# The setup of a two-layer attention kernel: laid-out weights, a bias network in 4 pieces, bias lines by head group on two DMA queues

## The chip, the cores and the metric

One core of a Trainium2 chip. The metric is the device time of one execution in microseconds, the median over several runs; for a changed kernel it is set against runs of the kernel before on the same chip. A profile comes from one more execution.

## The reference

The input x is 8 elements of 256 channels by 32 x 32 positions (1024), all in fp32. Two layers follow each other.

```python
# layer 0, per element, 8 heads of 32 channels
xn   = (x - mean_c(x)) / sqrt(var_c(x) + eps) * gamma
q, k, v = split(w_qkv @ xn)                         # 256 x 1024 each
sim  = einsum('bhdi,bhdj->bhij', q, k) * scale + bias[None]
out0 = w_out @ (softmax(sim) @ v) + x
# the bias depends on the weights alone: a small network on relative positions
rel  = sign(rel) * log(abs(rel) + 1)                # (i, j, 2), 63 x 63 distinct pairs
h    = leaky(rel @ w0.T + b0); h = leaky(h @ w1.T + b1)   # 64 wide
bias = h @ w2.T + b2                                # 8 heads
# layer 1: one head, 1024 x 1024 scores, then a residual
f, g, hh = Wf @ x + bf, Wg @ x + bg, Wh @ x + bh
out  = gamma1 * (hh @ softmax(f.T @ g)) + x
```

## The kernel before

The core works through the 8 elements one after the other (`element(b, ...)` on each engine). An element has two groups of 4 heads, and a group has a rows phase of 32 tiles (PE: scores of 128 x 1024, L617 and L618; DVE: adds the bias and takes the minimum of the negated sum, L1037; ACT: exp with a sum, L836) and a columns phase of 32 tiles (L638, L1051, L853, L665). Layer 1 of the element before, and the normalisation and the k and q of group 0 of the next element, are laid between these tiles by hand-written tables. Each engine executes its instructions in program order, and semaphores join them.

q and k are each split into a high and a low part (ACT writes the high, DVE the low part into `st`), stored to DRAM (`q_out`, `k_out`) and loaded again in another layout (`q_in`, 6 DMAs; `k_in`, 3 DMAs). `st` is a single buffer: `high_q0` may only write after the k store has landed, and `high_k` of group 1 only after the q store of group 1. All DMAs are issued by SP, in one queue and one order.

The bias of a tile is read from `bias_lines` in SBUF, which is filled once, in the setup that this case is about:

1. SP loads x of element 0 and 22 weight tensors. PE transposes the weights (27 products, `tiles_to_turn`) and DVE copies them out of PSUM, with gamma multiplied into `wqkvT` (L884 to L898).
2. The bias network runs on 63 x 63 = 3969 relative positions in `MSTEPS = 9` pieces of 441 columns: three products on PE (L678, L685, L692), two bias additions on ACT (L816, L823), two leaky steps and a table write on DVE (L1005, L1012, L1017). At fixed steps the statistics of element 0 are put in between: mean and var products (L443, 4 each), centre, square, rstd, norm.
3. SP stores the table of 8 heads x 3969 to DRAM (L383), and then writes 32 "lines" (L387, DRAM to DRAM): line x holds, for 8 heads and 63 offsets, the 32 values that column x needs, 504 rows of 128 bytes. After the 17th, SP issues the k store of group 0, and after the 32nd the q store, then `k_in`, `q_in` and 32 loads of bias lines into SBUF (L396, 4 for each head). Beside this PE makes k and q of group 0 (`k0`, `q0`, L486).
4. PE makes its first tiles when `q_in` has landed; DVE takes the first when the four bias loads of head 0 have landed. SP's next entries are the q store and `q_in` of group 1, x of element 1, and the k store of group 1.

## Time and profile before

| | |
|---|---|
| median of 3 runs | 1823.52 us (1823.15 to 1825.76) |
| profiled execution, its own time | 1826.01 us |
| its span | 1824.2 us |
| mean granted clock of PE, as a share of full | 0.928 |
| busy: PE, DVE, ACT | 89%, 82%, 76% of the span |
| DMA | 122.48 MB, almost all on SP's queue |

An engine's share is a mean over the span; a setup and eight elements lie in it. "PEclk" is the clock that PE was granted, as a share of 2.4 GHz; it has the two levels 1.0 and 0.5. A product of fp32 operands appears in the profile as two MATMUL entries. The time of one execution is 1.8 us above its span.

### The profile page before, as it was taken

The page shows a single profiled execution, that of the slowest core. Times are in us where ns is not written, and L with a number is a line of the kernel's source. Part 1 is how long each engine was busy: PE and PEld are TensorE (multiplying, and loading weights), DVE is VectorE, ACT ScalarE, POOL GpSimd, SP SyncE. Part 2 cuts the span into 40 slices and gives each one's busy share as a digit, 9 for nine tenths or more (in the row PEclk, how much of TensorE's full clock was granted, in tenths as well). Part 3 has the DMA queues.
Part 4 walks back from the last instruction along what each step waited for, and adds up shares of the span by engine and source line. Part 5 has one row for each costly group of instructions (what it writes and reads, how often), then busy time and mean ns, then how long its engine had stood idle before and what let it go on. Part 6 is the DMA issues. An engine that isn't in the chain of part 4 may idle for free.

```text
span 1824.2 us, 18855 instructions
## 1 busy us (share of the span) xinstructions
PE 1617.4 (89%) x6033; PEld 762.3 (42%) x6033; DVE 1498.5 (82%) x2217; ACT 1387.4 (76%) x2043; POOL 0.2 (0%) x4
## 2 busy tenths in 40 slices
PE   6635889989998999989998999989998999989988
PEld 2123333535444453534444353534444353535424
DVE  4226889889898989889898989889898988889853
ACT  1215888888788888878888787878788787889753
POOL 0000000000000000000000000000000000000000
PEclk8657878999999999999999999999999999989999
DMA  1298022502034102502034102502034111500000
GB/s 59 57 207 211 1 59 70 151 1 58 16 113 116 51 9 83 159 3 58 4 125 116 47 13 74 158 12 59 1 111 133 36 23 63 144 15 1 26 22 23
DMA packets 59031, 122.48 MB, mean 67 GB/s; under 512 B 22507, under 2 KB 25131, under 8 KB 58923
## 3 DMA queue, kind: packets, MB, share of 16 engines
q1 hardware_dynamic: 58932, 121.28, 24.3%
q8 instruction: 48, 0.79, 0.2%
q14 instruction: 51, 0.41, 0.1%
HBM read 78.66 MB, written 44.13 MB: 67 GB/s over the span
## 4 chain that ended last, share of the span: by engine, by line
PE 51%; DVE 24%; issue 17%; DMA 3%; ACT 3%; SPq 2%; DVEq 0%; ACTq 0%
DVE biased L1037 13%; PE psum L563 9%; PE psum L638 9%; PE psum L665 8%; PE psum L617 6%; PE psum L443 5%; DVE biased L1051 5%; PE psum L618 4%; PE psum L486 3%; PE psum L520 2%; PE psum L496 1%; SPq L387 1%; DMA q_parts<-st 1%; ACT probs L853 1%; DVE probs L971 1%
## 5 line engine op out<-in xcount | busy, mean ns | idle before, releaser
L1037 DVE CUSTOM_DVE_ANT_0 biased<-psum,bias_lines_sb 128x1024 f32<-128x1024 f32 x512 | 617.0, 1222 | 161.4 <-PE psum L618 125.0
L836 ACT ACTIVATE biased<-biased,nmax 128x1024 f32<-128x1024 f32 x512 | 587.2, 1147 | 144.0 <-DVE nmax L1037 139.9
L1051 DVE TENSOR_TENSOR biased<-psum,bias_lines_sb 128x1024 f32<-128x1024 f32 x512 | 598.4, 1218 | 43.5 <-PE psum L638 32.5
L853 ACT ACTIVATE probs<-biased 128x1024 f32<-128x1024 f32 x512 | 536.5, 1056 | 127.1 <-DVE biased L1051 107.5
L638 PE MATMUL psum<-q_stack,k_stack 98*128 98x512 f32 x1024 | 393.6, 492 | 38.8 <-DVE nmax L1037 16.2
L617 PE MATMUL psum<-k_stack,q_stack 96*128 96x512 f32 x512 | 331.3, 647 | 89.5 <-DVE nmax L1037 48.4
L638 PEld LDWEIGHTS psum<-q_stack,k_stack 98*128 98x128 f32 x1024 | 179.2, 201 | 326.8 <-issue 152.8
L665 PE MATMUL psum<-probs,vT 128*32 128x512 f32 x2048 | 283.0, 622 | 6.1 <-DVE st L926 3.9
L617 PEld LDWEIGHTS psum<-k_stack,q_stack 96*128 96x128 f32 x512 | 100.2, 196 | 274.0 <-DVE nmax L1037 175.2
L618 PE MATMUL psum<-k_stack,q_stack 96*128 96x512 f32 x512 | 212.1, 414 | 0.0
L563 PE MATMUL psum<-probs 128*128 128x512 f32 x384 | 186.6, 592 | 0.0
L618 PEld LDWEIGHTS psum<-k_stack,q_stack 96*128 96x128 f32 x512 | 102.7, 201 | 50.6 <-issue 47.3
L486 PE MATMUL psum<-xn,wqkvT 128*128 128x512 f32 x128 | 77.3, 698 | 26.3 <-DVE st L920 15.3
L836 ACT ACTIVATION_READ_ACCUMULATOR biased<-biased,nmax 128x1 f32 x512 | 96.1, 188 | 0.0
L563 PEld LDWEIGHTS psum<-probs 128*128 128x128 f32 x384 | 72.6, 189 | 46.4 <-issue 36.1
L665 PEld LDWEIGHTS psum<-probs,vT 128*32 128x32 f32 x2048 | 42.4, 109 | 101.3 <-issue 74.4
L784 ACT ACTIVATE probs<-probs,nmax 128x1024 f32<-128x1024 f32 x48 | 54.9, 1144 | 16.4 <-DVE probs L983 15.6
L443 PE MATMUL psum<-xn,wqkvT 128*128 128x512 f32 x128 | 66.8, 603 | 0.0
L496 PE MATMUL psum<-wqkvT,xn 128*128 128x256 f32 x256 | 65.7, 378 | 0.0
L532 PE MATMUL psum<-whT,x 128*128 128x256 f32 x256 | 65.5, 380 | 0.0
L508 PE MATMUL psum<-o,woutT 128*128 128x512 f32 x128 | 64.4, 593 | 0.8 <-ACT o L805 0.8
L563 PE MATMUL psum<-o,probs 128*128 128x512 f32 x128 | 64.8, 592 | 0.0
(86 smaller groups left out, 1148.2 us busy)
## 6 DMA issues: line engine op xcount, KB each, us to landing
k_stack<-k_parts SPq DMA_DIRECT2D x48, 512.0 KB, 7.3
q_stack<-q_parts SPq DMA_DIRECT2D x96, 256.0 KB, 5.7
k_parts<-st SPq DMA_DIRECT2D x16, 1024.0 KB, 4.5
q_parts<-st SPq DMA_DIRECT2D x16, 1024.0 KB, 3.9
xn<-in_x_dram SPq DMA_DIRECT2D x8, 1024.0 KB, 8.2
x<-in_x_dram SPq DMA_DIRECT2D x8, 1024.0 KB, 9.1
out_dram<-x SPq DMA_DIRECT2D x8, 1024.0 KB, 4.1
bias_lines_sb<-bias_lines SPq DMA_DIRECT2D x32, 240.0 KB, 23.7
```

The costliest lines, as they stand in the source:

```text
L443: mm = pe.matmul(psum[0:rows, bank + half, :], lhsT(k), src[:, k, half * HALF:(half + 1) * HALF], start=(k == 0), stop=(k == KC - 1))
L486: mm = pe.matmul(psum[:, bank, :], wqkvT[:, k, t * C:t * C + P], xn[:, k, half * HALF:(half + 1) * HALF], start=(k == 0), stop=(k == KC - 1))
L496: mm = pe.matmul(psum[:, 4 + arg % 2, 0:C], xn[:, k, arg * P:(arg + 1) * P], wqkvT[:, k, 2 * C:3 * C], start=(k == 0), stop=(k == KC - 1))
L563: mm = pe.matmul(psum[:, 4 + 2 * c + half, :], hs[:, t % HS, c * P:(c + 1) * P], attn1[t % 3][:, half * HALF:(half + 1) * HALF], start=(t ...
L617: pe.matmul(psum[:, bank, :], lhsT, back(keys, 0, HALF, N), start=True, stop=True)
L618: pe.matmul(psum[:, bank + 1, :], lhsT, back(keys, HALF, HALF, N), start=True, stop=True).then_inc(SEMS["a_mm"], 1)
L638: mm = pe.matmul(psum[:, bank + i, :], k_stack[:, g, 2 * j + i, t * P:(t + 1) * P], q_stack[:, g, NHALF - 1 - half, 2 * j + i, ::-1], star ...
L665: mm = pe.matmul(psum[h * HD:(h + 1) * HD, 4 + half, :], vT[:, t, (g * HG + h) * HD:(g * HG + h + 1) * HD], probs[:, ((q - PV_LAG) * HP + ...
L836: nc.scalar.activation(biased[:, m % BIASED, :], biased[:, m % BIASED, :], ACT.Exp, scale=-1.0, bias=nmax[:, m:m + 1], accum_out=rowsum[:, ...
L853: nc.scalar.activation(probs[:, n % P_SLOTS], biased[:, n % BIASED, :] .rearrange("p (i n) -> p i n", i=2), ACT.Exp).then_inc(SEMS["probs_ ...
L1037: nc.vector.tensor_tensor_reduce(biased[:, m % BIASED, :], pair(bank_of(g, first, ("rows", m))), bias_lines[:, g * HG + h, a0:a0 + N], -1. ...
L1051: nc.vector.tensor_tensor(biased[:, n % BIASED, :].rearrange("p (i n) -> p i n", i=2), psum[:, bank:bank + 2, :], bias_lines[:, g * HG + 2 ...
```

## The change

The host lays the weights out as the products want them (`laid_out`), so that the transposes and their copies are gone; only the product with gamma stays on DVE, now in place on `wqkvT` (two instructions of 128 x 768). The bias network works on two halves of the positions at once: 2 x 64 = 128 partitions with block-diagonal weights (`twice`), 4 pieces of 504 columns. The two halves share the middle row of offsets, and the table is stored in two DMAs. Lines are kept by group of 4 heads (`lines_dram[g, x]`, 252 rows of 128 bytes each): those of group 0 are issued half by SP and half by ACT, those of group 1 all by SP, after the bias loads of group 0. ACT now issues the later constants at the start, its 16 lines, and the k and q stores and loads of group 0 of element 0. The memset of two rows of `k_stack` goes from DVE to GpSimd. Nothing is changed in the elements but that the DMA helpers take the issuing engine as an argument.

```diff
-    lines_dram = nc.dram_tensor("bias_lines", [W, G * HG, DY, W], F32)
+    lines_dram = nc.dram_tensor("bias_lines", [G, W, HG, DY, W], F32)
...
-        MSTEPS = 9
-        MC = DY * DX // MSTEPS
+        HPT = G * HG
+        MROWS = (DY + 1) // 2
+        MSTEPS = 4
+        MC = MROWS * DX // MSTEPS
...
+        def lines_out(eng, g, x, done):
+            src = table_dram.ap().rearrange("h (a w) -> h a w", w=DX)[g * HG:(g + 1) * HG, :, W - 1 - x:2 * W - 1 - x]
+            eng.dma_start(lines_dram.ap()[g, x], src).then_inc(done, 16)
...
         def _(sp):
+            sp.dma_start(mlp, mlp_in).then_inc(mlp_loaded, 16)
+            sp.dma_start(rel_sb, rel_in).then_inc(mlp_loaded, 16)
             sp.dma_start(xn[:], x_dram[0]).then_inc(x_loaded, 16)
+            sp.dma_start(wqkvT[:], wqkv_in).then_inc(weights_loaded, 16)
+            sp.dma_start(gamma_col[:], gamma_in).then_inc(weights_loaded, 16)
...
             sp.wait_ge(table_ready, MSTEPS)
-            sp.dma_start(table_dram.ap(), table_sb).then_inc(table_stored, 16)
-            sp.wait_ge(table_stored, 16)
+            sp.dma_start(table_dram.ap()[:, 0:MROWS * DX], table_sb[0:HPT]).then_inc(table_stored, 16)
+            sp.dma_start(table_dram.ap()[:, MROWS * DX:DY * DX],
+                         table_sb[HPT:2 * HPT, DX:MROWS * DX]).then_inc(table_stored, 16)
+            sp.wait_ge(table_stored, 32)
+            for x in range(0, W, 2):
+                lines_out(sp, 0, x, lines_stored)
+            sp.wait_ge(lines_stored, 16 * W)
+            bias_in(0)
             for x in range(W):
-                src = table_dram.ap().rearrange("h (a w) -> h a w", w=DX)[:, :, W - 1 - x:2 * W - 1 - x]
-                sp.dma_start(lines_dram.ap()[x], src).then_inc(lines_stored, 16)
-                if x == W // 2:
-                    k_out(0, 0)
-            q_out(0, 0)
-            k_in(0, 0)
-            q_in(0, 0, ("s_mm", -1, SN))
-            sp.wait_ge(lines_stored, 16 * W)
+                lines_out(sp, 1, x, late_lines_stored)
+            sp.wait_ge(late_lines_stored, 16 * W)
+            bias_in(1)
...
         def _(pe):
-            pe.wait_ge(weights_loaded, 16 * N_WEIGHTS)
-            pe.wait_ge(consts_set, 1)
-            turned = 0
-            for src in tiles_to_turn((wq_raw, wo_raw, wh_raw), (wf_raw, wg_raw), (w0_raw, w1_raw, w2_raw)):
...
-            pe.wait_ge(rel_loaded, 16)
+            pe.wait_ge(mlp_loaded, 32)
...
         def _(act):
             nc.scalar.preload_act_table_set("natural_log_exp_and_others")
+            n = 0
+            for dst, src in ((ident[:], ident_in), (woutT[:], wout_in), (whT[:], wh_in), (wfgT[:], wfg_in),
...
+            do("rstd", 0, 0, 1, True, False)
+            do("rstd", 1, 0, 1, True, False)
+            act.wait_ge(table_stored, 32)
+            for x in range(1, W, 2):
+                lines_out(nc.scalar, 0, x, lines_stored)
             for kind, arg in (("high_k0", 0), ("high_k0", 1), ("high_q0", 0), ("high_q0", 1)):
                 do(kind, arg, 0, 1, True, False)
+                if (kind, arg) == ("high_k0", 1):
+                    k_out(nc.scalar, 0, 0)
+            q_out(nc.scalar, 0, 0)
+            k_in(nc.scalar, 0, 0)
+            q_in(nc.scalar, 0, 0, ("s_mm", -1, SN))
+            act.wait_ge(consts_loaded, 16 * N_CONSTS)
```

The first place is SP's queue between the table store and x of element 1. `bias_table` is the table in DRAM, `bias_lines` the lines there, `bias_lines_sb` those in SBUF. In the kernel before it reads:

```order
L383 DMA bias_table<-bias_lines_sb 8x3969
L387 DMA bias_lines<-bias_table 504x32 x17
L335 DMA k_parts<-st 128x2x1024
L387 DMA bias_lines<-bias_table 504x32 x15
L335 DMA q_parts<-st 128x2x1024
L362 DMA k_stack<-k_parts 32x4x1024 x3
L348 DMA q_stack<-q_parts 32x4x512 x6
L396 DMA bias_lines_sb<-bias_lines 32x1920 x32
L335 DMA q_parts<-st 128x2x1024
L348 DMA q_stack<-q_parts 32x4x512 x6
L407 DMA xn<-in_x_dram 128x2x1024
```

The same stretch of SP's queue in the changed kernel, where `probs` holds the table in SBUF:

```order
L367 DMA bias_table<-probs 8x2016
L368 DMA bias_table<-probs 8x1953
L330 DMA bias_lines<-bias_table 252x32 x16
L362 DMA bias_lines_sb<-bias_lines 32x1920 x16
L330 DMA bias_lines<-bias_table 252x32 x32
L362 DMA bias_lines_sb<-bias_lines 32x1920 x16
L298 DMA q_parts<-st 128x2x1024
L311 DMA q_stack<-q_parts 32x4x512 x6
L387 DMA xn<-in_x_dram 128x2x1024
```

The stores and loads of k and q of group 0 have left the queue; the q store of group 1 stands behind the lines and bias loads of group 1.

The second place is ACT between the end of the network and the first tile. L749 and L745 are `high_k0` and `high_q0`, L836 is the exp of a tile. Before:

```order
L823 ACTIVATE bias_lines_sb<-psum,probs 64x441 x2
L749 ACTIVATE st<-psum 128x512 x2
L745 ACTIVATE st<-psum 128x512 x2
L836 ACTIVATE biased,rowsum<-biased,nmax 128x1024 x4
L755 COPY vT<-psum 128x256
```

And in the changed kernel, where L716 and L712 are rstd, L732 and L728 are `high_k0` and `high_q0`, and L829 is the exp:

```order
L716 ACTIVATE o<-psum,eps_col 128x1024
L712 ACTIVATE o<-o 128x1024
L330 DMA bias_lines<-bias_table 252x32 x16
L732 ACTIVATE st<-psum 128x512 x2
L298 DMA k_parts<-st 128x2x1024
L728 ACTIVATE st<-psum 128x512 x2
L298 DMA q_parts<-st 128x2x1024
L325 DMA k_stack<-k_parts 32x4x1024 x3
L311 DMA q_stack<-q_parts 32x4x512 x6
L829 ACTIVATE biased,rowsum<-biased,nmax 128x1024 x4
```

ACT now issues 16 lines between rstd and the first `high_k0`, and 11 DMAs for k and q before its first tile.

## Rows read from the trace of the kernel before

**Rows 1.** The page: span, and busy time of the engines.

```profile
span 1824.2 us, 18855 instructions
...
PE 1617.4 (89%) x6033; PEld 762.3 (42%) x6033; DVE 1498.5 (82%) x2217; ACT 1387.4 (76%) x2043; POOL 0.2 (0%) x4
```

**Rows 2.** Stretches: length, busy us (entries) by engine, PEclk, DMA share, GB/s.

```profile
20.70:67.60 46.90, 45.42 (x70) 9.32 (x70) 20.75 (x31) 14.85 (x22) 0.00 (x0) 0.65 0.00 0
...
71.30:84.50 13.20, 4.03 (x9) 1.48 (x7) 1.38 (x2) 1.19 (x2) 0.00 (x0) 0.76 0.49 72
...
108.00:123.50 15.50, 2.07 (x4) 1.16 (x4) 0.05 (x1) 0.00 (x0) 0.00 (x0) 0.50 1.05 219
...
411.00:617.00 206.00, 191.15 (x748) 92.43 (x744) 183.35 (x270) 171.50 (x254) 0.00 (x0) 0.98 0.23 67
```

**Rows 3.** Timeline of ACT and DVE: start, us, what, [idle before, releaser].

```profile
89.20 0.60 ACT L745 ACTIVATE st<-psum 128x512 fp32r<-128x512 f32 x1 [14.96 <-DMA k_parts<-st]
...
123.45 1.22 DVE L1037 CUSTOM_DVE_ANT_0 biased<-psum,bias_lines_sb 128x1024 f32<-128x1024 f32 x1 [27.67 <-DMA bias_lines_sb<-bias_lines]
...
157.35 1.23 DVE L916 TENSOR_TENSOR st<-psum,st 128x1024 fp32r<-128x1024 f32 x1 [6.21 <-ACT st L741]
...
171.35 1.23 DVE L1037 CUSTOM_DVE_ANT_0 biased<-psum,bias_lines_sb 128x1024 f32<-128x1024 f32 x1 [7.21 <-PE psum L618]
```

**Rows 4.** Timeline of PE, same columns.

```profile
13.82 5.42 PE L437 MATMUL psum<-ident,probs 128*128 128x128 f32 x27 [13.82 <-DMA bfg<-in_L_conv_bg_dram]
...
46.91 0.95 PE L678 MATMUL psum<-bias_lines_sb,probs 2*64 2x441 f32 x2
47.79 0.95 PE L685 MATMUL psum<-bias_lines_sb,probs 64*64 64x441 f32 x2
...
90.67 3.75 PE L486 MATMUL psum<-xn,wqkvT 128*128 128x512 f32 x4 [15.34 <-DVE st L920]
...
118.12 0.79 PE L617 MATMUL psum<-k_stack,q_stack 96*128 96x512 f32 x1 [23.70 <-DMA q_stack<-q_parts]
...
168.24 2.08 PE L443 MATMUL psum<-xn,mean_w 128*128 128x512 f32 x2 [6.11 <-DMA xn<-in_x_dram]
```

**Rows 5.** Timeline of SP's queue: start, us, what, number of issues.

```profile
12.09 0.43 SPq L328 DMA_DIRECT2D bfg<-in_L_conv_bg_dram  x1
...
67.63 0.28 SPq L383 DMA_DIRECT2D bias_table<-bias_lines_sb  x1
71.25 13.21 SPq L387 DMA_DIRECT2D bias_lines<-bias_table  x17
84.51 0.58 SPq L335 DMA_DIRECT2D k_parts<-st  x1
...
97.40 0.58 SPq L335 DMA_DIRECT2D q_parts<-st  x1
...
105.64 16.71 SPq L396 DMA_DIRECT2D bias_lines_sb<-bias_lines  x32
140.50 0.39 SPq L335 DMA_DIRECT2D q_parts<-st  x1
...
159.01 0.39 SPq L407 DMA_DIRECT2D xn<-in_x_dram  x1
```

**Rows 6.** Groups of 20.7 to 67.6 us by form, PE: busy us, mean ns | idle.

```profile
L678 PE MATMUL psum<-bias_lines_sb,probs 2*64 2x441 f32 x18 | 11.9, 765 | 1.5 <-DVE probs L898 1.5
...
L443 PE MATMUL psum<-st,mean_w 128*128 128x512 f32 x8 | 5.3, 821 | 0.0
L443 PE MATMUL psum<-xn,mean_w 128*128 128x512 f32 x8 | 5.0, 773 | 0.0
```

**Rows 7.** The page, DMA issues: times, KB each, median us to landing.

```profile
q_parts<-st SPq DMA_DIRECT2D x16, 1024.0 KB, 3.9
```

More of the change, by code:

```diff
@@ L337, in q_out @@
-            def q_out(b, g):
-                need(sp, "lo_ready", b, split(g, 0))
-                need(sp, "q_loaded", b, g * Q_DMAS)
-                through_dram(q_dram, q_stored)
-            def q_in(b, g, done):
-                need(sp, "q_stored", b, 16 * (g + 1))
-                need(sp, *done)
-                for r, part in enumerate((0, 0, 1)):
-                    for half in range(NHALF):
-                        sp.dma_start(q_stack[r * HD:(r + 1) * HD, g, half].bitcast(F32),
-                                     q_dram.ap()[part, :, :, half * HALF:(half + 1) * HALF]
-                                     .rearrange("h d n -> d h n")).then_inc(q_loaded, 16)
@@ L695, in _ @@
                     if step == at:
+                        if kind == "mean":
+                            pe.wait_ge(consts_set, 1)
                         for quantum in range(QUANTA):
@@ L865, in _ @@
                 do(kind, arg, b, 1, False, False, tail=True)
+        @block.gpsimd
+        def _(pool):
+            nc.gpsimd.memset(k_stack[KS:KS + 2].bitcast(F32), 1.0).then_inc(ones_set, 1)
         @block.vector
@@ L1095, in shape_constants, with by_partition, twice, laid_out @@
     dy, dx = np.meshgrid(line, line, indexing="ij")
-    return [np.stack([dy.ravel(), dx.ravel()]), np.eye(P, dtype=np.float32)]
+    rows = side
+    parts = [a[half * (side - 1):half * (side - 1) + rows].ravel() for half in range(2) for a in (dy, dx)]
+    return np.stack(parts)
+def by_partition(w):
+    t = np.ascontiguousarray(w.T)
+    return t.reshape(t.shape[0] // P, P, t.shape[1]).transpose(1, 0, 2)
+def twice(w):
+    rows, cols = w.shape
+    both = np.zeros((2 * rows, 2 * cols), np.float32)
+    both[:rows, :cols] = w
+    both[rows:, cols:] = w
+    return both
+def laid_out(ins):
+    w0, b0, w1, b1, w2, b2 = (ins["L0_conv_cpb_" + n] for n in ("w0", "b0", "w1", "b1", "w2", "b2"))
+    d0, heads = w0.shape[0], w2.shape[0]
+    mlp = np.zeros((2 * d0, 2 * d0 + 2 * heads + 3 + 2 * d0), np.float32)
+    at = 2 * d0
+    mlp[:, 0:at] = twice(w1.T)
+    mlp[:, at:at + 2 * heads] = twice(w2.T)
+    mlp[:, at + 2 * heads] = np.concatenate([b1, b1])
+    mlp[0:2 * heads, at + 2 * heads + 1] = np.concatenate([b2, b2])
+    mlp[:, at + 2 * heads + 2] = np.concatenate([b0, b0])
+    mlp[0:4, at + 2 * heads + 3:] = twice(w0.T)
+    parts = KS_PARTS
+    wfg = np.stack([np.concatenate([by_partition(ins[n])] * parts, axis=2) for n in ("L1_conv_Wf", "L1_conv_Wg")], axis=2)
+    bfg = np.stack([np.concatenate([ins[n]] * parts) for n in ("L1_conv_bf", "L1_conv_bg")], axis=1)
+    gamma = ins["L0_conv_gamma"].reshape(-1, P).T
+    return [("x", ins["x"]), ("mlp", mlp), ("rel", relative_grid(ins["x"].shape[2])),
+            ("wqkv", by_partition(ins["L0_conv_w_qkv"])), ("gamma", gamma), ("identity", np.eye(P, dtype=np.float32)),
+            ("wout", by_partition(ins["L0_conv_w_out"])), ("wh", by_partition(ins["L1_conv_Wh"])), ("wfg", wfg),
+            ("bfg", bfg), ("bh", ins["L1_conv_bh"]), ("gamma1", ins["L1_conv_gamma"])]
 def kernel(**inputs):
@@ L1104 @@
     arrays, args = {}, []
[L1105 to L1106 removed]
+    ins = {n: np.asarray(inputs[n]) for n in _INS}
+    named = [(n, np.ascontiguousarray(a)) for n, a in laid_out(ins)]
     for name, a in named:
```

222 lines of the change are left out of this document (89 added, 133 removed).

## The prediction

> **What bounds the kernel now.** I read the page first: PE is busy 89% of a 1824.2 us span, DVE 82%, ACT 76% [rows 1]. Then the table by stretch: an element in the middle costs 206 us with PE busy 191 and DVE 183 of it [rows 2]; the change leaves that loop alone. The setup is another matter. The first score tile is handed to DVE at 123.45 us, after DVE had idled 27.67 us for the bias lines [rows 3]. So I read the timeline of PE and of SP's queue up to there. Four links follow each other: weights and transposes (first product of the bias network at 20.7 us), network and statistics up to 67.6 us, with PE busy 45.4 of 46.9 us [rows 2], the table through DRAM into lines (32 issues, 71.25 to 97.4), and q and k through DRAM (97.40 to PE's first tile at 118.12) [rows 4, 5]. Whatever the setup loses here comes off the end one for one, since everything later waits for the first tile.
>
> Two later waits belong to it too. DVE idles 6.21 us before 157.35, because ACT may write st only when the q store issued at 140.50 has landed (about 156.2, behind 32 bias loads). It idles 7.21 us before 171.35, since PE waits 6.11 us for the next element's x, issued behind that store at 159.01 [rows 3, 4, 5].
>
> **The change, link by link.** Durations are those of the profiled execution (1826.0 us for a span of 1824.2); its own time is 0.14% above the median of 1823.5 us, and I take the savings off the median.
>
> *Loads and transposes.* PE starts 1.7 us after the last of 23 weight loads is issued (12.09 to 13.82), and the issues lie 0.5 us apart [rows 4, 5]. Now PE and ACT need the first two loads only: issued at 0.7 and 1.2, so 1.2 + 1.7, and 0.6 for rows of up to 8 KB: 3.5 us. The 27 transposes and DVE's copies go. 20.7 becomes 3.5: **-17.2**. x and wqkv follow in the same queue; they land while PE does the first products. DVE's 6.9 us memset moves to POOL, which nothing waits for before the first tile. DVE scales wqkvT in two instructions of 768 columns; by the width that is about 2 us, and PE has the four mean products to do meanwhile.
>
> *Network and statistics.* PE is the bound there. The eight statistics products took 5.0 + 5.3 us [rows 6] and stay. The rest of the 46.9 us is 36.6 us for 27 products of 441 columns, 11907 columns; now 12 of 504, 6048 columns, on more rows and partitions, which cost PE nothing. 36.6 x 0.508 = 18.6. With 1 us for the shorter pipeline (four pieces hide less of the ACT and DVE steps): 29.9, of which I take 29.5; table ready at 33 us: **-17.4**. This stretch ran at a mean granted clock of 0.65 [rows 2]; I assume the same mix of the two levels. At 1.2 GHz only, two passes of a 512-column product take 1.87 us (3.75 for two products) [rows 4]; all of the stretch at that level would be 35 us. At 2.4 GHz a 441-column product takes 0.88 us (46.91 to 47.79) [rows 4], so 12 x 1.0 + 8 x 0.86 = 19 us. Bounds -28 to -12.
>
> *Table store.* 67.63 to 71.25 is 3.6 us [rows 5]; one more issue of 0.3: **+0.3**. Stored at 36.9.
>
> *Lines.* Before: 32 issues of 504 rows, 17 of them in 13.21 us: 0.78 each, while the 16 DMA engines are busy 0.49 [rows 2, 5]. So issuing bounds them, not moving. Now 16 on SP and 16 on ACT, of 252 rows. The bias loads, of 32 rows, cost 16.71/32 = 0.52 [rows 5]. An issue of 252 rows is thus between 0.52 and 0.78; nearer by row count to the former, but nothing shows how it grows, so I take 0.62: 9.9 us, to 46.8 (bounds 8.3 and 12.5). The Trainium skill speaks against a gain here (DMA: Bandwidth & Descriptors, Issuing engines are not separate DMA queues): two issuers save only the sequencer's time, usually small beside the transfer. By that the first group's lines would need half of the 25 us, 12.5 instead of 9.9; the row contradicts it, as the engines were half idle.
>
> *Splitting k and q.* Before, this lay beside the lines. Now ACT does it after its 16 issues, so it is on the path: two ACT writes and DVE's low halves, 2.0 us, from 0.60 and the 1.5 us between 89.20 and 90.67; k store until ACT may go on, 84.51 to 89.20, 4.7; high_q0, low_q0, 1.5; the second half of q on PE, 3.75; its split, 1.3 [rows 3, 4, 5]. Sum 13.2, q store issued at 60.0. From table stored to there it is 23.1 us against 26.15: **-3.0**.
>
> *Through DRAM.* q store to first tile took 20.7 us (97.40 to 118.12) [rows 4, 5]. Now the 16 bias loads of group 0 (3.9 MB; at the 219 GB/s of [rows 2], 17.9 us) run on the other queue at the same time, before they stood behind. Below: nothing, as two queues overlap what one does in turn. Above: all of it in series. That is 3.9 + 3.1 MB (k and q in) at 219 GB/s, 32 us; the two stores at 3.9 us each [rows 7], 8 us; and 6 us for the lines of group 1 (32 x 0.78 x 0.49 / 2). With 2 us before the bias loads begin, it ends 48 us after ACT's last line issue, where my chain has 13.2 + 20.7 = 33.9: 14 us. I take **+4**: PE's first tile at 84.7.
>
> *First DVE instruction.* Before, 5.3 us after PE's first tile, for want of bias lines [rows 3, 4]. These now land long before: 1.3 us, the two products: **-4.0**. DVE starts at 86.0 against 123.45: **-37.4**.
>
> *The two waits.* SP: lines 0 done at 48; 16 bias loads issued to 56; 32 line issues of 0.62 to 76; landed 78; 16 bias loads to 86, moved by 97 to 101. SP's next, the q store of group 1, is wanted 17 us after DVE's start (140.50 - 123.45), at 103. So the queue is free, and it lands in 3.9 us [rows 7] instead of 15.7: the 6.2 us go. x is then issued 2.7 us later and lands within 9.2 (159.01 to 168.24): 16 us after the q store's issue, against 27.7 before. PE wants it 38.7 - 6.2 = 32.5 us after DVE's start and has it at 33: I keep 1 to 2 us, of 7.2. Sum of both: **-11** (bounds -13, and -3 if the lines of group 1 are late by 8 us).
>
> Sum: -37.4 - 11 = -48.4, so **1775 us**. The steady elements add nothing either way; the phase of the clock in them may shift the end by 2 us.
>
> **Rivals.**
> 1. *The transfers get in each other's way.* The upper bound above, or the two waits stay. For: DMA is busy 1.05 of the time from 108 to 123.5 us [rows 2], and two queues make no more engines. Against: while q and k are split, 13 us, the bias loads have the engines to themselves. +10 us on the path, up to +8 for the waits: 1785 to 1793. Chance 0.17.
> 2. *Issues of 252 rows on two queues are no faster than 504 on one.* If one generator serves both, 32 x 0.78 = 25 us instead of 9.9: +15, 1790. For: nothing shows two queues at once. Against: one queue's idle engines. Chance 0.08.
> 3. *Few DMA engines per line transfer.* A lines transfer used about 0.49 x 13.2 x 16 / (17 x 504) = 12 ns of one engine per row. Were the 252 rows dealt by their four heads to 4 engines, 63 rows each, the 32 transfers would take 0.76 us each on the same four: 24 us, +14: 1790. Against: the order of the program shows them as one dimension of 252 rows, like the 504 before. The Trainium skill (the same page, Why a DMA increments its semaphore by 16 and not by 1) has the number of engines as the largest divisor up to 16 of the slowest dimension; 252 gives 14, as 504 does. Chance 0.03.
> 4. *PE gets its full clock in the setup.* 19 us instead of 29 for network and statistics: -10, 1765; with an uncontended DMA, 1760. For: the last part of the old stretch had slow, regular products, and the new one has fewer stops. Against: PE was busy 97% of 46.9 us and was granted 0.65 on average [rows 2]. The Trainium skill (TensorE: Matmul & The Clock Gate, What you observe) has sustained activity releasing the full clock; by it -10 would be right, and the trace does not agree. Chance 0.09.
> 5. *Slower than before.* ACT now issues DMAs ahead of the split of k and q. 86.0 reaches 123.45 + 11 only if each of ACT's 16 line issues takes 3.0 us more, 3.65 us. The dearest issues shown are the old lines, 0.78 [rows 5]. Chance 0.02.
> 6. *Nothing moves the end* (the first tile waits for something not seen, and the setup's gain is given back): 0.01.
>
> **How the numbers follow.** My own forecast, 1766 to 1784, holds 0.60. Rivals 1 to 3 lie above it and 4 below; between 1763 and 1794 lie nine tenths of 1, 2 and 3 and more than half of 4, over eight in ten together. This kernel's measurement tells changes above some 0.2% (3.6 us) from none. Faster: 0.97; same: 0.01; slower: 0.02.
>
> **What would show it.** In the changed kernel's profile: first product of the network at 3 to 4 us; table store issued at 33 (28 to 38); 16 line issues on ACT in about 10 us; ACT's q store at 60; PE's first tile at 85 and DVE's first at 86, with no wait for bias lines; no 6 us gap of DVE before high_k's partner, and one of under 3 us at the next element's mean; from there 206 us per element. I am wrong if an issue on ACT costs 1 us or more, if q and k take over 30 us through DRAM beside the bias loads, if the lines of group 1 land after 100 us, or if the elements themselves change.

## The result, and the profile after

The changed kernel takes 1793.16 us (median of 4, 1792.25 to 1795.72), the kernel before beside it 1824.64 us (1823.15 to 1826.65): a ratio of 0.983, 95% interval 0.981 to 0.985. That is 31.5 us less. The time lies 0.8 us inside the outer range of 1763 to 1794, but outside the forecast's own 1766 to 1784, 18 us above its 1775, and at the top of rival 1 (1785 to 1793). The profiled execution has a span of 1790.7 us, against 1824.2 [rows 1].

The timeline of PE in the changed kernel, in the columns of [rows 4]:

```profile
4.17 3.72 PE L648 MATMUL psum<-x,o 4*128 4x504 f32 x4 [4.17 <-DMA x<-in_rel_dram]
...
19.37 1.11 PE L648 MATMUL psum<-x,o 4*128 4x504 f32 x2
...
86.38 0.77 PE L587 MATMUL psum<-k_stack,q_stack 96*128 96x512 f32 x1 [26.95 <-DMA q_stack<-q_parts]
...
136.29 2.07 PE L413 MATMUL psum<-xn,mean_w 128*128 128x512 f32 x2 [6.06 <-DMA xn<-in_x_dram]
...
158.80 0.70 PE L608 MATMUL psum<-q_stack,k_stack 98*128 98x512 f32 x2 [0.23 <-DVE nmax L1015]
```

The first product stands at 4.17 where it stood at 20.7, the first score tile at 86.38 where it stood at 118.12. The next element's mean products still wait 6.06 us for x, as before. L608 is the first product of the columns phase; before it stood at 191.89 us:

```profile
191.89 0.70 PE L638 MATMUL psum<-q_stack,k_stack 98*128 98x512 f32 x2 [0.23 <-DVE nmax L1037]
```

From there to the end of the span are 1632.3 us before and 1631.9 us now. So all of the gain and all of the loss lie ahead of that product, and it serves as the mark: 33.1 us earlier. (The two profiled executions lie 33.5 us apart, the medians 31.5; the difference is between executions of one kernel.)

ACT with its queue (ACTq), and DVE, in the timeline of the changed kernel:

```profile
32.74 12.91 ACTq L330 DMA_DIRECT2D bias_lines<-bias_table  x16
45.70 1.08 ACT L732 ACTIVATE st<-psum 128x512 fp32r<-128x512 f32 x2 [15.33 <-issue]
47.72 0.39 ACTq L298 DMA_DIRECT2D k_parts<-st  x1
...
60.82 0.38 ACTq L298 DMA_DIRECT2D q_parts<-st  x1
...
71.67 2.73 ACTq L311 DMA_DIRECT2D q_stack<-q_parts  x6
...
87.73 1.23 DVE L1015 CUSTOM_DVE_ANT_0 biased<-psum,bias_lines_sb 128x1024 f32<-128x1024 f32 x1 [26.94 <-PE psum L588]
125.45 1.22 DVE L886 TENSOR_TENSOR st<-psum,st 128x1024 fp32r<-128x1024 f32 x1 [10.62 <-ACT st L724]
139.40 1.23 DVE L1015 CUSTOM_DVE_ANT_0 biased<-psum,bias_lines_sb 128x1024 f32<-128x1024 f32 x1 [7.16 <-PE psum L588]
```

The first DVE tile stands at 87.73 (forecast 86.0), and no longer waits for bias lines. But the two waits that were to go are there: 10.62 us where [rows 3] has 6.21, and 7.16 where it has 7.21. SP's queue shows what is late:

```profile
29.87 0.30 SPq L367 DMA_DIRECT2D bias_table<-probs  x1
...
32.73 12.46 SPq L330 DMA_DIRECT2D bias_lines<-bias_table  x16
47.62 9.45 SPq L362 DMA_DIRECT2D bias_lines_sb<-bias_lines  x16
57.12 43.93 SPq L330 DMA_DIRECT2D bias_lines<-bias_table  x32
102.76 7.81 SPq L362 DMA_DIRECT2D bias_lines_sb<-bias_lines  x16
110.70 0.40 SPq L298 DMA_DIRECT2D q_parts<-st  x1
124.33 2.69 SPq L311 DMA_DIRECT2D q_stack<-q_parts  x6
127.11 0.40 SPq L387 DMA_DIRECT2D xn<-in_x_dram  x1
```

The 32 lines of group 1 took 43.93 us to issue; 20 were reckoned. So the bias loads of group 1 are issued at 102.76, just when the q store of group 1 is wanted, and that store, issued at 110.70, lands 13.6 us later, at 124.33. It took 3.9 us by [rows 7]. The chain of work that ended last goes through single line issues:

```profile
59.45 0.75 SPq L330
60.24 7.06 SPq L330
...
85.10 0.73 SPq L330
```

At 60.24 an issue takes 7.06 us instead of 0.75, and they stay slow until 85.10: that is from the q store of group 0 (issued at 60.82) to shortly before the landing of `q_in`. The table by stretch (columns as in [rows 2]) shows the DMA engines full both there and when the second q store is under way, a granted clock of 1.00 over the network, and an unchanged element:

```profile
4.10:29.10 25.00, 24.06 (x40) 7.25 (x40) 10.63 (x15) 8.05 (x11) 3.55 (x1) 1.00 0.25 93
32.70:45.60 12.90, 6.54 (x8) 2.52 (x8) 0.06 (x1) 0.00 (x0) 0.00 (x0) 0.63 0.53 71
...
60.80:86.40 25.60, 0.02 (x1) 0.05 (x1) 0.00 (x0) 0.00 (x0) 0.00 (x0) 0.53 1.05 243
...
110.70:124.30 13.60, 3.79 (x12) 1.51 (x10) 3.94 (x8) 2.76 (x6) 0.00 (x0) 0.74 0.93 242
411.00:617.00 206.00, 192.42 (x746) 93.21 (x745) 183.54 (x270) 171.88 (x254) 0.00 (x0) 0.97 0.24 67
```

The clock's 1.00 is not to be trusted for the first part. It reads 1.00 from 2.0 to 4.1 us too, before PE's first product. In the kernel before, the weight loads between the statistics products lie 0.85 us apart at a granted 0.51 (26.0 to 27.9) and 0.43 apart at 1.00 (28.4 to 30.1). Here they lie 0.85 apart up to 14.27 and 0.43 from 14.96: up to some 14.6 us PE worked at the pace of the lower level.

The theory from here on, **Q**: the bias loads of group 1 (16 of 240 KB, 3.9 MB) fill the DMA engines when the q store of group 1 and x of the next element are wanted; the first DVE tile itself came within 1.7 us of the forecast. Rivals of Q: the store is held up by its place in SP's queue and not by the engines; the head groups and the second queue cost nothing, or bring something, once this is mended; and it is the slow issue of the lines that must be cured.

### The profile page after: what moved, and what is told of

Its sections match the earlier page's. It is cut to its first block, busy times and chain, and to the rows that moved or that the text cites. A ratio compares the mean times of both kernels' runs of the same rounds, so it can differ in the third digit from the quotient of the medians.

```text
span 1790.7 us, 18676 instructions
## 1 busy us (share of the span) xinstructions
PE 1590.5 (89%) x5976; PEld 754.6 (42%) x5976; DVE 1478.0 (83%) x2168; ACT 1382.0 (77%) x2033; POOL 7.1 (0%) x5
## 4 chain that ended last, share of the span: by engine, by line
PE 49%; DVE 24%; issue 18%; SPq 3%; ACT 3%; DMA 2%; ACTq 1%; DVEq 0%
DVE biased L1015 13%; PE psum L533 9%; PE psum L608 9%; PE psum L635 8%; PE psum L587 5%; DVE biased L1029 5%; PE psum L413 5%; PE psum L588 4%; PE psum L456 3%; SPq L330 2%; PE psum L490 2%; PE psum L466 1%; ACT biased L829 1%; DMA xn<-in_x_dram 1%; ACT probs L846 1%
## 5 line engine op out<-in xcount | busy, mean ns | idle before, releaser
L829 ACT ACTIVATE biased<-biased,nmax 128x1024 f32<-128x1024 f32 x512 | 587.2, 1147 | 140.5 <-DVE nmax L1015 136.1
L608 PE MATMUL psum<-q_stack,k_stack 98*128 98x512 f32 x1024 | 393.5, 492 | 39.3 <-DVE nmax L1015 16.2
L608 PEld LDWEIGHTS psum<-q_stack,k_stack 98*128 98x128 f32 x1024 | 179.0, 201 | 328.2 <-issue 152.5
L829 ACT ACTIVATION_READ_ACCUMULATOR biased<-biased,nmax 128x1 f32 x512 | 96.2, 188 | 0.0
```

Of the source, the lines that this page charges most:

```text
L608: mm = pe.matmul(psum[:, bank + i, :], k_stack[:, g, 2 * j + i, t * P:(t + 1) * P], q_stack[:, g, NHALF - 1 - half, 2 * j + i, ::-1], star ...
L829: nc.scalar.activation(biased[:, m % BIASED, :], biased[:, m % BIASED, :], ACT.Exp, scale=-1.0, bias=nmax[:, m:m + 1], accum_out=rowsum[:, ...
```

## The experiments

Twelve kernels, each an edit of the changed kernel. The network up to the table store is the same in all of them, yet that store was issued between 27.5 and 30.4 us in their profiled executions. The difference lies ahead of the third product of L648, which starts at 16.34 in the changed kernel and at 13.95 in experiment 5, where the weight loads come closer together from 11.28 on and not from 14.96. So 2 to 3 us between two times can be scatter of the setup, and beside each time I read distances that are free of it: **A**, from the issue of the table store to the first DVE tile, **B**, from there to the first product of the columns phase, and **C**, from that to the end of the span. They are worked out from the timelines, in us. C lies between 1628.0 and 1636.6, mostly near 1632; what moves it is not traced, so a few us of a time can come from there too. The times are medians, and A, B and C are of one profiled execution each.

| kernel | A | B | C | its time |
|---|---|---|---|---|
| before | 55.8 | 68.4 | 1632.3 | 1824.6 |
| changed | 57.9 | 71.1 | 1631.9 | 1793.2 |
| 1: bias of group 1 late | 58.3 | 61.1 | 1630.2 | 1778.7 |
| 2: q store of group 1 on ACT | 58.2 | 69.1 | 1636.4 | 1792.8 |
| 3: lines of group 1 held | 58.1 | 83.1 | 1636.6 | 1808.7 |
| 4: first half of the change alone | 53.5 | 67.8 | 1632.1 | 1784.0 |
| 5: 4, bias late | 53.6 | 60.5 | 1632.3 | 1776.4 |
| 6: lines of group 0 on SP, bias late | 49.3 | 76.2 | 1628.0 | 1787.5 |
| 7: the same, bias early | 49.2 | 91.7 | 1633.5 | 1804.9 |
| 8: 256 rows a line | 55.7 | 69.5 | 1628.9 | 1786.4 |
| 9: 5, bias behind the shift rows | 53.6 | 55.5 | 1633.3 | 1773.3 |
| 10: 9, k and q on ACT | 52.1 | 56.3 | 1632.2 | 1771.7 |
| 11: changed, bias behind the shift rows | 58.6 | 55.5 | 1631.9 | 1778.6 |
| 12: 11, 256 rows | 55.7 | 55.6 | 1632.6 | 1773.3 |

**1. The bias loads of group 1 out of the way.** SP issues them behind the k store of group 1, where they are needed only for the next rows phase.

```diff
             sp.wait_ge(late_lines_stored, 16 * W)
-            bias_in(1)
...
                 k_out(sp, b, 1)
+                if first:
+                    bias_in(1)
                 k_in(sp, b, 1)
```

> The changed kernel with one edit: SP issues the 16 bias loads of group 1 only after the q store, q loads, x load and k store that follow them now. Theory Q (order in SP's queue): the q store of group 1 waits behind these loads, 13.6 us from issue to landing; ahead of them it lands in about 4 us. DVE's wait before the low part of k (10.6 us) goes, and the wait for the next element's x (7.2 us) shrinks to under 3; first tile unchanged at 87.7; time 1793 - 10.6 - 4 to 6 = 1777 to 1779 us. Theory B (the DMA engines are full, whatever the order): the loads are only moved, the store still takes over 8 us or the x load becomes late instead; 1788 to 1793 us. If the bias of group 1 becomes late, DVE waits for it at the start of group 1 (some 75 us after its first tile), which neither expects.

Measured: 1778.68 us (1778.18 to 1779.19), ratio 0.974 (0.971 to 0.977): 14.5 us below the changed kernel, as theory Q expected. The two profiled executions lie 13.3 apart, 10.0 of them in B, 2.0 in an earlier table store (27.89) and 1.7 in C. SP's queue and the first columns product:

```profile
103.52 0.39 SPq L298 DMA_DIRECT2D q_parts<-st  x1
107.44 2.96 SPq L311 DMA_DIRECT2D q_stack<-q_parts  x6
...
115.74 7.97 SPq L362 DMA_DIRECT2D bias_lines_sb<-bias_lines  x16
...
147.23 6.02 PE L609 MATMUL psum<-q_stack,k_stack 98*128 98x512 f32 x12 [5.49 <-DMA q_stack<-shift_rows]
```

The store lands in 3.9 us, PE waits 0.50 us for x instead of 6.06, and theory Q holds. In their place stands a smaller one: the shift rows of group 0 (`shift_to_stack`, L346) are now queued behind the bias loads, and the columns phase starts 5.49 us late.

**2. The q store of group 1 from ACT's queue.** If its place in SP's queue holds it up, another queue cures it.

```diff
             def element(b, first, last):
-                q_out(sp, b, 1)
+                if not first:
+                    q_out(sp, b, 1)
...
+                        if first and g == 0 and m == 10:
+                            q_out(nc.scalar, 0, 1)
```

> The changed kernel with one edit: ACT issues the q store of group 1 of element 0, after its 11th tile, so that it is in the other queue while the 16 bias loads of group 1 run in SP's. Theory Q (first in, first out within a queue): the store lands in 4 to 7 us, as ACT's k store did beside the bias loads of group 0 (6.6), instead of 13.6; DVE's wait of 10.6 us falls to 1 to 4. The q loads behind it start earlier too, but share with the bias loads. Time 1783 to 1787 us. Theory B (full engines): the store still takes 11 to 14 us in the other queue and the time stays at 1791 to 1794.

Measured: 1792.77 us (1790.37 to 1795.18), ratio 0.982 (0.978 to 0.985), the time of the changed kernel.

```profile
101.75 7.56 SPq L362 DMA_DIRECT2D bias_lines_sb<-bias_lines  x16
122.08 2.69 SPq L311 DMA_DIRECT2D q_stack<-q_parts  x6
...
108.42 0.44 ACTq L298 DMA_DIRECT2D q_parts<-st  x1
```

Issued 2.3 us earlier, the store lands at 122.08, after 13.7 us: as long as on SP's queue, and as theory B expected. DVE waits 7.02 us instead of 10.62, but C is 4.5 us longer. Another queue is no cure. The profile's view of the DMA queues (q1 is SP's, q10 ACT's; packets, MB, share of the 16 engines) shows what happens, first from 112 to 114 us, then from 118 to 120:

```profile
q1 hardware_dynamic: 90, 0.45, 103.7%
...
q10 hardware_dynamic: 83, 0.34, 52.0%
q1 hardware_dynamic: 81, 0.40, 50.6%
```

For the first 6.0 us, to 114.4, no packet of the store moves, while the bias loads keep the engines full (SP's queue at 101% of them from 108.4 to 113.5). From then on the two queues share the engines evenly. The 3.64 MB that both moved from 108.42 to 122.08 are the store and all that was left of the 3.9 MB of bias (1.36 MB had moved before): the store lands only when the bias loads are through. Why its first packet comes so late stays open. The Trainium skill (DMA: Bandwidth & Descriptors, Issuing engines are not separate DMA queues) says that transfers run on the same 16 engines and interleave, whichever engine starts them; the trace agrees from 114.4 us on. The same page (Queues, rings and completion order) has each DMA engine take turns between the queues that have work, packet by packet. If that meant half of the 242 GB/s for the store, an estimate, it would land in 8.7 us. From its first packet to its landing it took 7.7, with packets of 3.9 KB beside ones of 5.0 KB (272 for 1.05 MB, 511 for 2.57 MB); the 6.0 us ahead of that the rule does not give.

**3. Lines of group 1 held back until q is loaded.** This cures the slow issues, and tells whether the lines slow q and k.

```diff
             bias_in(0)
+            need(sp, "q_loaded", 0, Q_DMAS)
             for x in range(W):
                 lines_out(sp, 1, x, late_lines_stored)
```

> The changed kernel with one edit: SP starts the 32 line issues of group 1 only when the q loads of group 0 have landed, so no lines run beside k and q. If two queues slow each other (theory B), then k and q go through DRAM faster, first tile at 83 to 85 instead of 87.7 us, and the 32 issues take 0.77 us each, 25 us instead of 43.9, as the 16 of group 0 did. They end at about 111, the bias loads of group 1 follow, and the q store of group 1 is issued later than now, at 118 to 120: DVE's wait grows by 7 to 10 us. Time 1795 to 1801. If the slow issues (1 to 7 us each between 60 and 85 us) have another cause, they stay slow or the first tile does not move.

Measured: 1808.69 us (1807.35 to 1810.02), ratio 0.991 (0.988 to 0.993).

```profile
86.94 25.83 SPq L330 DMA_DIRECT2D bias_lines<-bias_table  x32
...
88.51 1.23 DVE L1016 CUSTOM_DVE_ANT_0 biased<-psum,bias_lines_sb 128x1024 f32<-128x1024 f32 x1 [27.11 <-PE psum L589]
137.62 1.22 DVE L887 TENSOR_TENSOR st<-psum,st 128x1024 fp32r<-128x1024 f32 x1 [22.18 <-ACT st L725]
```

The issues now take 0.81 us each instead of 1.37, with the DMA engines 0.28 busy instead of full: it is the full engines that stretch them. But the expectation missed otherwise: the first tile comes no earlier (A 58.1, a wait of 27.11 us against 26.94), and the time is 7.7 us above its range. So the lines of group 1 did not slow q and k. What does is the bias loads of group 0 beside them. From q store to PE's first tile it is 25.6 us in the changed kernel, 25.7 here and 24.2 or more in all kernels that issue these loads ahead of the q store; where they stand behind the q loads or come after, it is 20.2 to 20.8 (20.7 before, and experiments 4, 5, 6, 7, 9 and 10). In the changed kernel the q store, issued at 60.82, moves no packet before 66.5, as the store in experiment 2. All behind the lines is later here: the q store of group 1 is issued at 122.17, and its wait grows to 22.18.

**4. The first half of the change alone.** Laid-out weights and the four-piece network stay; lines, k, q and bias go back to SP in the order and shape of before.

```diff
-    lines_dram = nc.dram_tensor("bias_lines", [G, W, HG, DY, W], F32)
+    lines_dram = nc.dram_tensor("bias_lines", [W, G * HG, DY, W], F32)
...
             for x in range(W):
                 lines_out(sp, 0, x, lines_stored)
+                if x == W // 2:
+                    k_out(sp, 0, 0)
+            q_out(sp, 0, 0)
+            k_in(sp, 0, 0)
+            q_in(sp, 0, 0, ("s_mm", -1, SN))
+            sp.wait_ge(lines_stored, 16 * W)
+            bias_in(0)
+            bias_in(1)
```

> Weights laid out and the bias network in 4 pieces as in the changed kernel, but lines (504 rows, 32 issues on SP), k and q and bias loads in the queue and order of the kernel before. It splits the gain. The table is stored 37.4 us earlier than before (32.7 against 71.25 less the 1.1 of the second store), and nothing after that changes: first tile at DVE at 123.45 - 38.5 = 85 us, both waits (6.2 and 7.2) as before, time 1824.6 - 38.5 = 1786 us. That would mean that the second half of the change (head groups, two queues) costs 7 us net: its own chain through ACT's line issues and the crowded queues gain nothing at the first tile (87.7) and add 4 us to the wait for the q store. If instead the second half pays, as the prediction had it (-3.0 + 4 - 4 - 11 = -14), this kernel takes 1800 or more.

Measured: 1784.01 us (1783.07 to 1784.95), ratio 0.977 (0.974 to 0.980), 9.2 us below the changed kernel.

```profile
58.80 0.57 SPq L297 DMA_DIRECT2D q_parts<-st  x1
...
83.30 1.22 DVE L1008 CUSTOM_DVE_ANT_0 biased<-psum,bias_lines_sb 128x1024 f32<-128x1024 f32 x1 [25.66 <-DMA bias_lines_sb<-bias_lines]
117.39 1.23 DVE L879 TENSOR_TENSOR st<-psum,st 128x1024 fp32r<-128x1024 f32 x1 [6.81 <-ACT st L725]
```

The q store of group 0 comes at 58.80, sooner than the changed kernel's 60.82, though 32 issues of 504 rows stand ahead of it, since the split of k and q lies beside them again. A is 53.5 against 57.9, and the two waits are those of before (6.81 and 6.94). The expectation held within 2 us. So weights and network gave some 40 us, and head groups with two queues took 9.2 back by the medians. The two profiled executions lie 7.6 apart, 4.4 of them in A and 3.3 in B.

**5. The first half, with the bias loads of group 1 late.** Experiments 4 and 1 together; `bias_in(1)` goes behind the k store of group 1.

> The run e5 (laid-out weights and short network, then the lines, k and q in the order of the kernel before on SP alone) with the bias loads of group 1 moved behind the k store of group 1. Theory: the two waits of e5 (6.8 and 6.9 us of DVE) come only from the bias loads that stand ahead of the q store, whatever the head groups or the second queue do. First tile unchanged at 83 us, both waits under 2 us, 1784 - 11 to 13 = 1771 to 1773 us; that is below e1 (1778.7), so neither the lines by head group nor the second queue is needed for the gain. Rival: the waits come from elsewhere (the x load itself, 9 us), then only the first goes: 1777.

Measured: 1776.35 us (1775.59 to 1777.56), ratio 0.974 (0.972 to 0.975). The wait for the q store is gone, that for x is down to 2.13, and PE waits 5.07 us for the shift rows, as in 1. It gains 7.7 us on 4, with B 7.4 shorter. The waits came out nearly as expected, but the time is 3.4 us above the expected range, which had no wait for the shift rows in it.

**6. All lines of group 0 on SP, bias loads of group 1 late.** ACT keeps only the stores and loads of k and q.

```diff
-            for x in range(0, W, 2):
+            for x in range(W):
                 lines_out(sp, 0, x, lines_stored)
...
-            for x in range(1, W, 2):
-                lines_out(nc.scalar, 0, x, lines_stored)
```

> The changed kernel with the bias loads of group 1 moved as in e1, and all 32 lines of group 0 issued by SP; ACT issues k and q alone. In the changed kernel ACT's 16 line issues (12.9 us) stand ahead of the split of k and q and so on the path to the first tile. If that is what the second queue costs, ACT splits k at 33 to 38 us, its q store goes out at about 52 instead of 60.6, and the first tile comes at 76 to 79 us instead of 86.2: 1778.7 - 8 = 1769 to 1772. Lines of group 0 end later, at 59 (32 issues of 0.77), just before the q loads. Rival: lines and bias loads then fall into the time of the q loads and slow them, first tile at 83 or later and 1776 to 1779.

Measured: 1787.51 us (1784.42 to 1791.29), ratio 0.981 (0.979 to 0.982). A miss: 15.5 us above the expected range, and 8.5 above the rival's.

```profile
79.07 31.23 SPq L330 DMA_DIRECT2D bias_lines<-bias_table  x32
110.42 0.47 SPq L298 DMA_DIRECT2D q_parts<-st  x1
...
78.38 1.22 DVE L1013 CUSTOM_DVE_ANT_0 biased<-psum,bias_lines_sb 128x1024 f32<-128x1024 f32 x1 [27.70 <-DMA bias_lines_sb<-bias_lines]
115.66 1.22 DVE L884 TENSOR_TENSOR st<-psum,st 128x1024 fp32r<-128x1024 f32 x1 [9.59 <-ACT st L725]
```

The first tile came at 78.38, 8 us before that of 1, as expected (A 49.3). But SP was then issuing the lines of group 1 until 110.3, past the time at which the q store was ready, and the store waited for its sequencer. Here it is the place in the queue that costs.

**7. The same with the bias loads of group 1 where the change has them.**

> As e7, but with the bias loads of group 1 where the changed kernel has them. The first tile is earlier (76 to 79), but the lines of group 1 are issued later (from 68 us), so that the bias loads of group 1 start at about 103 or later and the q store of group 1 is wanted at 95: DVE waits 20 us or more for it. 1790 to 1796: the gain at the first tile is given back in full at the q store.

Measured: 1804.85 us, a single execution. The first tile comes at 77.82; the q store is issued at 119.56 and takes 14.6 us, and DVE waits 29.59 us. A wait of 20 us or more was expected, and came; the time is 9 to 15 us above what was expected. The late lines and the full engines add up.

**8. 256 rows in a line transfer instead of 252.**

```diff
-            src = table_dram.ap().rearrange("h (a w) -> h a w", w=DX)[g * HG:(g + 1) * HG, :, W - 1 - x:2 * W - 1 - x]
+            src = table_dram.ap().rearrange("h (a w) -> (h a) w", w=DX)[LINE_AT[g]:LINE_AT[g] + LROWS,
+                                                                        W - 1 - x:2 * W - 1 - x]
```

> The changed kernel with 256 rows in each line DMA instead of 252 (the four more rows belong to a neighbouring head and are not read). An issue of 504 rows took 0.77 us in the kernel before, one of 252 rows takes 0.77 too, and one of 32 to 256 rows in 16 equal shares 0.45: so rows do not set it. Theory D (how the rows divide): 252 and 504 divide by 14 but not by 16; with 256 rows an issue takes about 0.46, the 16 issues of ACT 7.4 instead of 12.9 us, and the first tile comes 5 us earlier: 1788 us. Theory R (rows of 128 bytes from DRAM to DRAM are dear by themselves): 0.77 as before, 1793 us.

Measured: 1786.35 us, a single execution.

```profile
33.28 10.71 SPq L333 DMA_DIRECT2D bias_lines<-bias_table  x16
...
33.28 10.43 ACTq L333 DMA_DIRECT2D bias_lines<-bias_table  x16
```

An issue took 0.66 us where one of 252 rows took 0.79, so 2 us less in all for four more rows (2.2 in A). Row count alone would make it longer. Neither theory gave this size (0.46 and 0.77), and of the 6.8 us by which the time is lower, A and B hold 3.7. The Trainium skill (DMA: Bandwidth & Descriptors, Why a DMA increments its semaphore by 16 and not by 1) lets the number of engines divide the slowest dimension, 16 for 256 rows and 14 for 252. If the issue time went down by 14/16, which the page does not say and is my estimate, it would be 0.69; 0.66 is near it. That the number of engines is the cause is argued from three counts (504 and 252 rows alike, 256 less), not shown.

**9. The bias loads behind the shift rows.** The kernel of 5, with `bias_in(1)` moved once more.

```diff
                 for r in range(NHALF):
                     shift_to_stack(b, 0, r)
+                if first:
+                    bias_in(1)
```

> The kernel of the run before (laid-out weights and the four-piece network, lines, k, q and bias of group 0 all on SP in the order of before, bias loads of group 1 late), with these bias loads moved once more, from ahead of k_in of group 1 to behind the four stores of the shift rows of group 0. Theory: the 5 us that PE waits for q_stack<-shift_rows at the start of the columns phase are the price of having the bias loads ahead of those stores. Then that wait falls to under 1 us, nothing new is late (bias lines of group 1 are issued at about 156, landed by 172, wanted at about 183) and the time is 1770 to 1773. Rival: the stores wait for something else (ACT's shift rows), and the time stays at 1776.

Measured: 1773.27 us (1772.93 to 1773.92), ratio 0.972 (0.970 to 0.973), 3.1 us below 5 and 0.3 above the expected range.

```profile
119.39 33.21 SPq L345 DMA_DIRECT2D q_stack<-shift_rows  x4
152.65 7.54 SPq L361 DMA_DIRECT2D bias_lines_sb<-bias_lines  x16
...
137.83 0.71 PE L610 MATMUL psum<-q_stack,k_stack 98*128 98x512 f32 x2 [0.23 <-DVE nmax L1009]
```

The columns phase starts without a wait, and nothing is late behind it. B is 55.5 us. Of the 12.9 us that it is shorter than in the kernel before, nothing came from the setup's own work.

**10. As 9, with k and q of group 0 on ACT's queue.**

```diff
-                if x == W // 2:
-                    k_out(sp, 0, 0)
-            q_out(sp, 0, 0)
-            k_in(sp, 0, 0)
-            q_in(sp, 0, 0, ("s_mm", -1, SN))
...
+                if (kind, arg) == ("high_k0", 1):
+                    k_out(nc.scalar, 0, 0)
+            q_out(nc.scalar, 0, 0)
+            k_in(nc.scalar, 0, 0)
+            q_in(nc.scalar, 0, 0, ("s_mm", -1, SN))
```

> As the other kernel of this call, and also the k and q stores and loads of group 0 are issued by ACT; the 32 lines of 504 rows stay on SP in one piece, and ACT issues none. Theory: the second queue is worth something for k and q, since in the order of before the k store stands behind 17 lines (43.6 for an operand ready at 36.7). Now k store at 37, q store at 50 instead of 56.8, lines landed at 57, PE's first tile at 71 to 74, and DVE's first tile, which then waits for the bias lines of head 0, at 74 to 78 instead of 81: 1764 to 1769. Rival: the DMA engines are full from 58 us on whatever the order (7 MB of k, q and bias at some 230 GB/s), then the first DVE tile stays at 80 to 81 and the time at 1770 to 1773.

Measured: 1771.70 us (1770.00 to 1772.42), ratio 0.971 (0.969 to 0.972), the fastest, though its interval meets that of 9. The rival expectation was right on the time; its first DVE tile came 1 to 2 us later than it said.

```profile
32.89 40.28 SPq L329 DMA_DIRECT2D bias_lines<-bias_table  x32
...
73.12 0.76 PE L584 MATMUL psum<-k_stack,q_stack 96*128 96x512 f32 x1 [22.18 <-DMA q_stack<-q_parts]
...
82.14 1.23 DVE L1009 CUSTOM_DVE_ANT_0 biased<-psum,bias_lines_sb 128x1024 f32<-128x1024 f32 x1 [29.84 <-DMA bias_lines_sb<-bias_lines]
```

PE's first tile comes 5.0 us earlier than in 9, at 73.12, but the lines beside k and q took 40.28 us to issue instead of 25.5, and DVE waits for the bias lines until 82.14. What the second queue gives to q it takes from the lines.

**11 and 12. The changed kernel with the bias loads behind the shift rows,** with 252 rows (11) and with 256 (12).

> The changed kernel as it is (head groups, two queues), with the bias loads of group 1 behind the four stores of the shift rows of group 0. Theory: both mends of the order add up, -14.5 for the q store and x and -5 for the shift rows: 1773 to 1775, the same within measurement as 1773.3 of the kernel with one queue, ungrouped lines and the same mend. Then head groups and two queues are worth nothing by themselves. Rival: the second half costs something by itself, since its first tile comes at 86 and not at 82: 1776 to 1778.

> As the other kernel of this call, with 256 rows in each line transfer instead of 252 (some rows of the middle head are stored in both groups and not all are read). The 16 issues on each queue then take 10.5 us instead of 12.9, as seen before. Theory: with the late bias loads out of the way these 2.4 us reach the end: 1771 to 1773. Rival: the q store of group 0 and the loads behind it are bound by the full DMA engines, the first tile stays at 86 and the time within 1 us of the other kernel.

Measured: 11 takes 1778.58 us (1775.48 to 1778.77), ratio 0.974 (0.973 to 0.976); 12 takes 1773.34 us (1771.78 to 1774.04), ratio 0.971 (0.970 to 0.973). In 11 the wait for the shift rows is gone, and B is 55.5 as in 9, against 61.1 in experiment 1. Its profile is of its fastest execution, with the table store at 27.63; that the median stands 3 us above it, and level with experiment 1, is of the size of the setup's scatter, but there is no trace of the other three executions to show it. Whether moving the loads from behind the k store to behind the shift rows is worth anything to the time of the changed kernel is therefore not shown; in the kernel of 5 it was worth 3.1 us. Against 9, the head groups and the second queue cost 5.0 us of A (58.6 and 53.6) and 5.3 us of the time. Of these, 12 gives 2.9 back in A (55.7), as its theory said, and its time is that of 9. The rival expectation of 11 was right, and more so than it said.

## Why the prediction was right, and where not

That the setup's gain reaches the end, and where it comes from, was right. That the time still fell inside the outer range is luck: with the network as reckoned (17.4 us and not 21.2) the time would have been 1797, above the range. The terms, as measured in the two profiled executions, add up to the 33.1 us of the mark within 0.1.

*Loads and transposes.* Forecast -17.2, measured -16.5: first product at 4.17 instead of 3.5.

*Network and statistics.* Forecast -17.4, measured -21.2 (46.9 to 25.7, from 4.17 to 29.87). The assumed mix of clock levels was wrong. The profile grants 1.00 over the stretch, where it had 0.65 [rows 2], and by the distances of the weight loads PE was at the lower pace up to some 14.6 us and at the full one from there. Rival 4 had the direction right and the size wrong: not 19 us but 25.7. About 4.6 of the 6.7 us are the lower pace (the first six entries of 504 columns took 0.93 to 1.03 us each, where later ones took 0.55, and the first eight entries of the statistics 5.69 us, where the last eight took 3.70; an estimate from these rows), 0.85 is a wait for x, and 0.8 lies between the last product and the store. The prediction's bound for the lower level, 35 us, should have been 37 by its own rows (12 products at 1.84, 8 at 1.87); its bound of -12 would then have been -10.

*Table store.* +0.3 forecast, -0.8 measured (29.87 to 32.73).

*Lines.* The term of 9.9 us was too small: 12.9, just above its upper bound. An issue costs 0.78 to 0.81 us with 252 rows as with 504, so the row count that I went by says nothing; the number of engines that it divides by fits what was measured (experiment 8). Rival 3 is out: 32 transfers in 12.9 us and not 24, with the DMA engines 0.53 busy, where four of 16 could be 0.25 at most. But two queues issue side by side: 32 lines in 12.9 us, where one queue took 25.8 in experiment 3. So rival 2 was right on an issue and wrong on the queues, and the rule that the prediction quotes from the Trainium skill (a second issuer saves only the sequencer's time) agrees with the trace: here that time was the bound, and 12.9 us are near the 12.5 that the prediction worked out by it.

*Splitting k and q.* 13.2 forecast, 15.1 measured (45.70 to 60.82), the difference being the k store: 6.6 us instead of 4.7 beside the bias loads. With the lines, from table stored to q store is 28.1 us against 26.15, so this part of the change cost 1.9 where -3.0 was forecast: the second queue shortens the lines to half, but puts the split behind them, and that had been free before.

*Through DRAM and first DVE instruction.* Forecast +4 and -4.0, measured +4.8 (25.6 against 20.7) and -4.0. The cause was the one named, the bias loads of group 0 (experiment 3).

*The two waits.* This step failed. It forecast -11 and measured +2.6: 35.7 us won at the first DVE tile, 33.1 at the first columns product. (The first wait grew by 4.4 us and the second stayed; the rest of that stretch took 1.8 less.) It said "16 bias loads issued to 56; 32 line issues of 0.62 to 76; landed 78; 16 bias loads to 86". The first was right (57); the 32 issues ended at 101. Of the 24 us that these issues took beyond the forecast, 5 are the price of one (0.77, not 0.62) and 19 are 8 issues between 60.24 and 85.10, which took 24.9 us instead of 6.2, beside the q and k loads and the bias loads of group 0. I had counted these transfers against q and k, but not against the lines in the other queue. Experiment 3 shows the price of an undisturbed issue, 1 shows that the bias loads at 103 were all that held up store and x, and 2 that a place in another queue does not get the store past them. One sign of being wrong that the prediction named came true (the lines of group 1 landing after 100 us), and its bound for lines that are late, by 8 us, was too tame: they were late by 24. It was rival 1 in its second half, that the waits stay; on the path it had 14 us where 4.8 were measured.

*The elements, and rivals 5 and 6.* An issue on ACT costs 0.81 us and not 3.65, and the setup's gain is at the end. No change forecast; 1632.3 and 1631.9 us from the mark to the end. Right.

## What to carry to other kernels

In a setup with a long list of transfers, date each by when it is needed and not by when its source is ready: the 3.9 MB of bias for group 1 were asked for at 102.8 us, when an urgent 1 MB store needed the engines, and the first tile that reads them stands at 204.1. Moving these 16 loads behind the shift rows took 15.5 us out of B and 14.6 off the time (experiment 11). When work moves to a second queue, count two things: what on that engine now stands behind the issues, and the time of an issue beside full engines, not in an empty queue.

## What the hardware showed beyond that

- An issue of a DRAM-to-DRAM line transfer takes 0.78 us with 504 rows, 0.78 to 0.81 with 252 and 0.66 with 256, undisturbed; beside full engines single ones take 1 to 7 us (60.24 to 85.10).
- A 1 MB store takes 3.9 us alone and 13.6 to 14.6 when 16 loads of 240 KB have just been issued, on their queue or on the other (experiment 2). On the other queue its first packet moves only after 6.0 us.
- Bias loads alone moved some 220 GB/s (110.5 to 114 us in experiment 2), a store beside them and they together 375 (116 to 120).
- The granted clock reads 1.00 from the start of the changed kernel's profile, even while PE stands idle; the first six entries of 504 columns took 0.93 to 1.03 us each and later ones 0.55. So the clock at the very start is better read from the distance of equal products. The table store scatters by 3 us (27.5 to 30.4) between kernels that are alike up to there, mostly with the moment at which that distance halves (14.96 in the changed kernel, 11.28 in experiment 5): the first eight entries of the statistics took 5.69 us in one and 4.12 in the other.
